# Loading the residual rows of x inside the next batch's pass, with GpSimd's loop written out

## The reference

```
x = layernorm(x + attention(x))            # 16 heads of 16 columns, causal
x = layernorm(x + moe(x))                  # for batch 0 only does moe add expert outputs here

attention: q, k, v = split(x @ qkv_w.T); rotary on q and k
  heads 0..5    softmax(q k / 4) v
  heads 6..9    softmax(1 / (eps + acosh(-c * inner) / sqrt(c))) v      # "hyperbolic"
  heads 10..15  softmax(4 * cosine(q, k)) v
  y = concat(heads) @ proj_w.T + proj_b
```

## Time and profile before

| | before |
|---|---|
| median of 3 runs | 2035.73 us |
| lowest, highest | 2028.61, 2038.44 us |
| the profiled execution, device time | 2027.79 us |
| its span in the profile | 2026.2 us |
| TensorE busy | 1621.9 us (80%) |
| ScalarE busy | 1391.7 us (69%) |
| VectorE busy | 1194.5 us (59%) |
| GpSimd busy | 820.5 us (40%) |

### The profile page before, as it was taken

The page is one execution under the profiler, slowest core; times in us unless marked ns, Lnnn a source line. Parts: engine busy times, 40 slices in busy tenths (PEclk is TensorE's granted clock), DMA queues, the critical chain, the costliest instruction groups (busy, mean ns, idle before and its releaser), DMA issues. The chain is left out here.

```text
span 2026.2 us, 38980 instructions
## 1 busy us (share of the span) xinstructions
PE 1621.9 (80%) x13082; PEld 912.6 (45%) x13082; DVE 1194.5 (59%) x3014; ACT 1391.7 (69%) x1456; POOL 820.5 (40%) x497
## 2 busy tenths in 40 slices
PE   7999858878976997798689778978977997618993
PEld 4665513334433443444334334434433443418993
DVE  5886746536854776576568567765865775421113
ACT  3665648887886888788778878888887888401110
POOL 3334424344443544544444445445444655300003
PEclk9999969889987998899799889978997998759997
DMA  4699731451065015505420650254055101149862
GB/s 163 199 246 293 224 107 52 88 91 34 2 106 117 12 18 92 116 12 74 112 49 2 105 117 12 31 90 114 2 85 126 47 21 43 43 160 413 319 239 73
DMA packets 66079, 215.18 MB, mean 106 GB/s; under 512 B 16944, under 2 KB 26800, under 8 KB 57104
## 3 DMA queue, kind: packets, MB, share of 16 engines
q1 hardware_dynamic: 56704, 179.35, 34.7%
q0 software_dynamic: 9200, 33.43, 5.3%
HBM read 144.14 MB, written 68.58 MB: 105 GB/s over the span
## 5 line engine op out<-in xcount | busy, mean ns | idle before, releaser
L1153 ACT ACTIVATE a_PT<-a_s 128x1024 f32<-128x1024 f32 (+3 forms) x576 | 460.0, 809 | 177.8 <-PE a_s L972 110.0
L969 PE MATMUL a_s<-Q,K 96*128 96x512 bf16 (+7 forms) x1152 | 331.4, 352 | 101.3 <-ACT a_PT L1153 71.9
L1231 POOL TENSOR_TENSOR a_Z<-a_Z,a_R 128x2182 f32<-128x2182 f32 x64 | 290.2, 4535 | 147.5 <-ACT a_R L1165 147.3
L1228 POOL TENSOR_TENSOR a_R<-a_Z 128x2182 f32<-128x2182 f32 x64 | 245.0, 3829 | 257.0 <-DVE a_Z L1350 192.4
L1358 DVE TENSOR_REDUCE a_mx<-a_w 128x1 f32<-128x512 f32 (+2 forms) x576 | 307.7, 550 | 55.9 <-PE a_w L997 42.5
L984 PE MATMUL a_o<-a_PT,a_V 128*32 128x512 f32 (+3 forms) x2304 | 268.7, 541 | 75.7 <-ACT a_PT L1153 46.8
L1350 DVE TENSOR_SCALAR_CACHE_REDUCE a_Z<-a_w 128x512 f32<-128x512 f32 (+7 forms) x384 | 202.3, 529 | 133.7 <-PE a_w L1012 94.1
L1029 PE MATMUL a_w<-a_ident,a_R 128*128 128x128 f32 (+1 forms) x1152 | 208.8, 309 | 19.0 <-POOL a_R L1238 7.7
L1404 DVE COPY a_PTh<-a_w 128x512 f32<-128x512 f32 (+1 forms) x256 | 157.6, 620 | 106.4 <-PE a_w L1029 101.9
L997 PE MATMUL a_w<-K,Q 96*128 96x512 bf16 (+2 forms) x576 | 187.7, 334 | 31.1 <-DVE a_mx L1358 9.7
L969 PEld LDWEIGHTS a_s<-Q,K 99*128 99x128 bf16 (+1 forms) x1152 | 112.1, 103 | 196.0 <-ACT a_PT L1153 109.2
(11 more groups left out here) (165 smaller groups left out, 2575.6 us busy)
## 6 DMA issues: line engine op xcount, KB each, us to landing
e_w<-in_w SPq DMA_DIRECT2D x23, 2048.0 KB, 8.7
qk_parts<-p_parts SPq DMA_DIRECT2D x128, 192.0 KB, 3.3
Q<-qk_parts SPq DMA_DIRECT2D x144, 128.0 KB, 5.3
K<-qk_parts SPq DMA_DIRECT2D x144, 128.0 KB, 7.1
v_rows<-p_vt SPq DMA_DIRECT2D x8, 2048.0 KB, 9.7
a_V<-v_rows SPq DMA_DIRECT2D x32, 512.0 KB, 8.7
p_xT<-in_xt SPq DMA_DIRECT2D x8, 1024.0 KB, 8.2
a_X<-in_x POOLq DMA_DIRECT2D x8, 1024.0 KB, 16.3
```

Of the source, the lines that this page charges most:

```text
L969: m = pe.matmul(sB[x % 2][:, i, 0:w], Kb[0:r, h, P * j:P * j + P], Qb[0:r, h, t0:t0 + w], start=True, stop=not diag)
L1153: act.activation(PT[:, u % 2, 2 * k:2 * k + 2, 0:w], sB[x % 2][:, :, 0:w], ACT.Exp, scale=scale_of(GROUPS[g][2 * k])).then_inc(prob.sem, 1)
L1228: pool.tensor_tensor(r, z, z, ALU.mult).then_inc(z_sq.sem, 1)
L1231: pool.tensor_tensor(z, z, r, ALU.add).then_inc(z_sum.sem, 1)
```

## The change

`rows_in` moves from quarter step 141 of a batch's own pass to quarter step 20 of the next pass, which is 23 quarter steps later. It becomes a LATE item. It keeps the wait for `rows_out` of the batch before, now inside `rows_in`. `shift` moves from quarter step 25 to 34. For the last batch `rows_in` is issued after the last pass, ahead of the tail. The wait needs a batch number that is a Python number, and GpSimd's loop over the middle passes becomes a Python loop, so that its instructions are written out six times; the loops of the other engines stay.

```diff
-        for at, item in ((25, ("shift",)), (104, ("variance", 0)), (106, ("inverse_root", 0)),
+        for at, item in ((34, ("shift",)), (104, ("variance", 0)), (106, ("inverse_root", 0)),
...
-                         (131, ("normalize", 1, 0)), (132, ("normalize", 1, 1)), (133, ("rows_out",)), (141, ("rows_in",))):
+                         (131, ("normalize", 1, 0)), (132, ("normalize", 1, 1)), (133, ("rows_out",)), (20, ("rows_in",))):
...
         LATE = ("turn_rows", "project", "statistics", "variance", "inverse_root", "newton", "normalize", "add_bias", "mid_out",
-                "rows_out", "shift")
+                "rows_out", "shift", "rows_in")
...
             def rows_in(b):
+                if b:
+                    hold(pool, out_sent.sem, out_sent.at(b - 1), pool_passed)
                 pool.dma_start(X[:], io["x"][bass.ds(b, 1)].rearrange("o (n p) c -> p (o n) c", p=P)) \
                     .then_inc(x_here.sem, 16)
...
                     rows_out(d, io["out"], 1, out_sent)
+                elif kind == "rows_in":
+                    rows_in(d)
...
                     for slot in step:
                         for item in slot:
-                            if item[0] == "rows_in":
-                                if not is_first:
-                                    hold(pool, out_sent.sem, out_sent.at(b - 1), pool_passed)
-                                rows_in(b)
-                            elif not is_late(item):
+                            if not is_late(item):
                                 do(b, b, item)
                             elif not is_first:
                                 do(b, b - 1, item)
...
                     if is_last and u % 4 == 3 and u // 4 < NT:
                         spread_rows(u // 4)
+                if is_last:
+                    rows_in(b)
...
-            with nc.Fori(1, B - 1, engines=[pool.engine], hint_back_edge=True) as b:
+            for b in range(1, B - 1):
                 turn(b)
```

## The result

The changed kernel takes 2042.4 us (median of 20 runs, 2031.7 to 2058.5), the kernel before 2029.85 us in 20 runs on the same chip. The ratio of the runs is 1.0051, 95% interval [1.0032, 1.007]; the quotient of the two medians alone is 1.0062. 2023.4 us was predicted, with a range of 2010 to 2040. The prediction had only three runs of the kernel before, and their median, 2035.73 us, is 5.9 us above that of the 20. The profiled execution of the changed kernel took 2045.68 us and its span is 2043.9 us, 17.7 us more than the span before.

What follows compares the result with a forecast made beforehand. No engine is full inside a pass; idle time lies in TensorE's waits for group 3, 27.0 us. Terms -17.3 - 1.0 + 6.0, the others 0, give -12.3 us: 2035.7 to 2023.4 us, range 2010 to 2040.

Steps and rivals of the forecast that it cites:

- Step 1: Pass starts: with X's load gone, TensorE waits less for group 3; -17.3 us, bounds nothing and 27.0 us.
- the first one: Starts 3, 5, 6 and 7: group 3 lands as X's main part ends, so all four waits go; 5.1 us.
- Rival A: Pass starts: group 3 keeps its lateness without X; 2035.6 us, or 2040.7 if no waits go; chance 0.30.
- The second term: Starts 1, 2 and 4: the few X packets beside group 3 cost at most their whole engine time; 12.2 us.
- Step 2: Quarter step 141: GpSimd's wait for the old rows and the issue go; -1.0 us, bounds 0 and 3.0.
- Steps 3 and 4: Quarter steps 20 and 34: X lands in 5.9 to 7 us, `shift` fits before the first mask; 0 us.
- Rival C: Quarter step 20: X lands late, delaying the first mask and `add_root` of unit 1; 2066.8 us; chance 0.06.
- Step 6: GpSimd's loop written out: idle time covers the branch and code fetch; 0 us, bounds -2 and +4.
- Step 5: Tail of the last batch: `shift` waits for X, delaying the mask TensorE waits for; +6.0 us, bounds 5 and 10.

Runs made afterwards that it cites:

- 8 KB first, same tail: Small loads first, bias addition behind the tail's masks: on the kernel before, 0.9973; on the changed kernel, also with the last batch's X loaded early, 0.9892.

## Why the prediction was wrong

Side by side (ratio; the seven passes in us). The ratios are of 6 to 23 runs; the passes are of one profiled execution each and carry its luck. In the row with group 2 held one profiled execution was 9.2 us above its median and the other 5.7 below; in the last row they were 1.4 above and 8.4 below. So up to 15 of the 24.0 us and 10 of the 21.9 may be of the executions.

| loads of group 3 and 2 | X at the pass start | X at quarter step 20 | passes, difference |
|---|---|---|---|
| as they are | 1 (1291.9); loop written out 1.0001 (1287.3) | 1.0051 (1297.2) | +5.3 or +9.9 |
| 8 KB loads first | 0.9994 (1283.3) | 0.996 (1270.2) | -13.1 |
| group 2 held | 0.9929 (1286.7) | 0.99 (1262.7) | -24.0 |
| 8 KB first, same tail | 0.9973 (1288.3) | 0.9892 (1266.4) | -21.9 |

*Step 1, -17.3 us, is the step that failed.* The waits for group 3 went from 27.0 to 24.8 us in sum, and a kernel whose X was still at the pass start had 19.0. The term that broke it is the first one, that at the starts 3, 5, 6 and 7 the wait ends with X and so goes with it, 5.1 us. These four waits grew by 9.9 us, to 14.94. It was argued from X having 72.3% of the engines when the wait ends. That X was there was true; that nothing else would be was not. SyncE issues group 2 and its values close behind the last small load, and when X leaves, their packets take its share and run beside the same twelve small loads. The step named this as its lower bound ("group 2 then simply starts earlier and takes X's place"). Group 2 did not start earlier, but it took the place. Rival A gave that 2035.6 to 2040.7 us with a chance of 0.30, and it should have been the forecast. The rows for it stood in the trace: in starts 1, 2 and 4 group 3 went on with hardly any of X on the engines.

The second term, 12.2 us at the starts 1, 2 and 4, came in size: 12.1 us in this pair of profiles. In the three profiles with X moved and the loads as they were, these starts have 9.8, 8.8 and 9.3 us of waits, in the two with X at the start 21.9 and 16.2. For the other four starts it is 14.9, 12.9 and 17.5 against 5.1 and 2.8. Its reason is not shown: it was a bound taken as a value, and no row has those 33 packets hold anything up. So a gain in one group of starts was paid back in the other, and the step as a whole bought nothing that the times show.

What X costs shows only where the other cause is gone: by the ratios, and with the 6 us that the late X of the last batch costs in the tail added back, 7 + 6 = 13 us where the 8 KB loads go first and 6 + 6 = 12 where group 2 is held; 16 us where the tails are alike. In the first two pairs the intervals overlap (by the medians the first is 3 + 6); in the third, 0.9973 [0.995, 0.9996] against 0.9892 [0.9852, 0.9931], they do not, and this pair carries the finding. So the 17.3 us were near the size of the second of two causes that overlap. That is luck: they were added up for a kernel in which X's move by itself gave nothing.

The Trainium skill says in "DMA: Bandwidth & Descriptors", section Queues, rings and completion order, that an engine takes the descriptors of one ring in their order. An order alone says nothing of how long a packet takes. Who reads it as a promise that group 2, issued later on the same queue as group 3, can't hold group 3 up, would expect nothing of the hold; it gained 1.5% (1.0051 to 0.99), so by the measurement transfers behind a load on the same queue slow it. The same page, section Why a DMA increments its semaphore by 16 and not by 1, gives as the number of engines of such a load the largest number up to 16 that divides the slowest dimension of both its sides, and puts it on the lowest-numbered ones. By that the twelve loads of one partition would go to the same few engines, one after the other. The trace agrees as far as it goes: with group 2 held, one engine's worth of the 16, 6.3%, carried ten of them one after the other. No view has the engine's number. Why a packet takes 0.98 us and not 0.32 when all engines are loaded stays open.

*Step 2* was right about the mechanism and the cover. GpSimd's wait for `out<-a_X` is gone. It lay under TensorE's wait for group 3, and since that stayed, nothing came of it. With group 2 held it costs TensorE 2.90 + 1.57 = 4.5 us at two starts; it is a part of what X's move is worth there.

*Steps 3 and 4* hold: landings of 5.9 to 6.4 us, `shift` behind `square` of unit 1. X would have been in time until 1237.91 - 4.54 - 1223.18 = 10.2 us after its issue, so it had 3.8 us or more to spare against the 3 to 4 forecast. Rival C did not come. *Step 6* holds: 1.0001.

*Step 5* was forecast at 6.0 us. The wait is 12.45 - 6.52 = 5.93 us longer, and 12.43 in the run with the small loads first. The tail grew by 9.1 us in the profile. The 3.2 us beyond do not need the change: idle time before the second transposes and longer transposes after it (1.51 us and 3.84 us for 18 in the changed kernel) stand in the run with the loop alone too, with an unchanged wait for the mask. Against that run the tail grew 76.7 - 71.4 = 5.3 us, and with group 2 held 74.1 - 69.5 = 4.6. The prediction had taken the 67.6 us of one profile for the tail's length.

In sum: 0 for steps 1 and 2, 0 for 3, 4 and 6, and 6 us for step 5 give 2035.7 + 6.0 = 2041.7 us, beside the 2042.4 measured. That they meet is luck, because 2035.7, the median of three runs, lies 5.9 us above that of the 20. The change cost 10.4 us by the ratio (0.51% of 2035.7) and 12.5 by the medians of 20 runs, so 4 to 7 us of it are not in this sum. The profiles put them into the passes, which are 5 to 10 us longer in the changed kernel than in the two kernels with X at the start; two more runs with X moved and the loads as they were have 1295.8 and 1300.1 us. Their waits for `t_parts`, 21.7 and 26.8 us, lie in the range of the others. TensorE's busy time in the passes is 1062.0, 1065.2 and 1062.3 us in the three with X moved, and 1055.7 and 1058.7 in the two with X at the start, for the same work. But the kernel before with group 2 held has 1062.0 too, so this does not come with X's move alone, and its cause was not found.

## What to carry to other kernels

When a load is late, list everything that is issued on any queue up to its landing, and ask of each transfer that is taken away which one will take its share of the DMA engines, even if that one is issued no earlier; a wait that two transfers cause is taken away by moving the load itself, or by holding back all that comes behind it. Small loads that many instructions wait for belong ahead of the large ones of the same group. And a load that a pass hides easily is not hidden in the iteration that has no next pass: the last one should keep its old place.

## What the runs showed of the hardware

Twelve loads of 8 KB, issued behind twelve of 128 KB and ahead of group 2, needed 12.7 us from the last issue to the start of the work that waited for them, with the 16 engines 87.7% busy; with nothing issued behind them it was under 6.0 us. Issued first, the same loads kept nothing waiting. That later transfers on the same queue delay earlier ones by 6 us was not expected. What is seen of it is that each packet takes longer: 0.98 us on average where all 16 engines are loaded and 0.32 us where the small loads are alone, one at a time on one engine.

TensorE's clock in the tail rises at different points in executions of nearly the same code. In the changed kernel the granted clock is 0.50 (1.2 GHz) throughout the 8.7 us after its wait for the mask, and 0.89 on average in the 10 us after that:

```profile
1761.30:1770.00 8.70, 5.95 (x26) 5.08 (x27) 3.60 (x12) 2.67 (x4) 0.82 (x2) 0.50 0.01 2
1770.00:1780.00 10.00, 8.83 (x110) 7.44 (x108) 6.41 (x16) 0.00 (x0) 0.01 (x1) 0.89 0.02 4
```

and those of the kernel before, from the same point of the tail on:

```profile
1748.30:1757.00 8.70, 7.26 (x50) 6.27 (x54) 5.85 (x16) 4.08 (x5) 0.82 (x2) 0.70 0.00 0
1757.00:1767.00 10.00, 6.83 (x96) 5.50 (x89) 5.25 (x16) 0.00 (x0) 0.00 (x0) 1.00 0.02 5
```

Full speed is 2.4 GHz. In the changed kernel TensorE stood 12.45 us before the first of these stretches, in the kernel before 6.52 us; but the run with the loop alone also stood 6.52 us and had the slow transposes, so that alone does not decide it. What does was not tried.
